# The last layer's two attentions as one stream of 32 tiles, with its norms and MLP weights made inside the stream

## What is computed

```python
def _L3_xattn_ref(hidden_states, encoder_states, ltor_mask, cross_mask, ln1_s, ...):
    ln_out = layernorm(hidden_states, ln1_s, ln1_b)
    qkv = ln_out @ w_qkv + b_qkv
    q, k, v = jnp.split(qkv, 3, axis=-1)
    ctx = merge_heads(attention(split_heads(q), split_heads(k), split_heads(v), ltor_mask))
    x = hidden_states + ctx @ w_ao + b_ao
    ln_out = layernorm(x, ln2_s, ln2_b)
    q = ln_out @ w_q + b_q
    kv = encoder_states @ w_kv + b_kv
    k, v = jnp.split(kv, 2, axis=-1)
    ctx = merge_heads(attention(split_heads(q), split_heads(k), split_heads(v), cross_mask))
    x = x + ctx @ w_co + b_co
    ln_out = layernorm(x, ln3_s, ln3_b)
    return x + gelu(ln_out @ w1 + b1) @ w2 + b2
```

## Time and profile before

| | |
|---|---|
| median of three runs | 1942.26 us (1941.73 to 1946.75) |
| the profiled execution | 1941.19 us, span from first to last instruction 1939.5 us |
| mean granted clock of PE | 0.942 of full |
| busy: PE, PEld, DVE, ACT, POOL | 89%, 76%, 52%, 51%, 22% |
| layer 3 begins, its MLP begins, the span ends | 1510.1, 1824.2, 1939.5 us |

### The profile page before, as it was taken

One profiled execution on the slowest core, in us unless ns is written; L12 is line 12 of the kernel. 1 busy time (PEld: TensorE's weight loads), 2 busy tenths in 40 slices (PEclk: granted clock), 3 DMA queues, 4 the chain that ended last, 5 costly groups with the idle time before them and its releaser, 6 DMA issues. The chain is left out here.

```text
span 1939.5 us, 36373 instructions
## 1 busy us (share of the span) xinstructions
PE 1731.0 (89%) x14350; PEld 1470.4 (76%) x14350; DVE 1002.6 (52%) x2150; ACT 998.8 (51%) x1890; POOL 431.9 (22%) x399
## 2 busy tenths in 40 slices
PE   5999999999979999999998598899489689699597
PEld 4888889888858888898887488577366467567486
DVE  6444444444364444444443733677678566667633
ACT  4545555455435555555554344566457476476443
POOL 5000000000020000000000300345510377377400
PEclk7999999999979999999999799899789799799799
DMA  4000000000020000000000100000100000100101
GB/s 153 23 22 22 0 22 22 22 22 0 1 67 23 22 22 0 22 22 22 22 0 1 47 0 8 21 2 2 52 1 0 26 2 2 36 2 2 47 0 44
DMA packets 55049, 39.77 MB, mean 21 GB/s; under 512 B 11891, under 2 KB 54451, under 8 KB 54963
## 3 DMA queue, kind: packets, MB, share of 16 engines
q1 hardware_dynamic: 54962, 38.57, 6.7%
HBM read 36.46 MB, written 2.10 MB: 20 GB/s over the span
## 5 line engine op out<-in xcount | busy, mean ns | idle before, releaser
L689 DVE TENSOR_TENSOR l0a_c_lo<-l0a_c_ps,l0a_c_hi 128x512 fp32r<-128x512 f32 x128 | 88.6, 692 | 267.2 <-ACT l0a_c_hi L643 267.2
L631 ACT ACTIVATE l0a_weight_t<-l0a_t_ps 64x256 f32<-64x256 f32 x256 | 96.8, 378 | 230.7 <-PE l0a_t_ps L532 229.2
L728 DVE TENSOR_TENSOR x<-l0a_o_ps,x 128x1024 f32<-128x1024 f32 x64 | 78.4, 1225 | 202.9 <-PE l0a_o_ps L102 202.9
L552 PEld LDWEIGHTS l0a_c_ps<-l0a_weight_t,l0a_v 128*128 128x128 f32 x1024 | 135.3, 193 | 14.4 <-ACT l0a_weight_t L631 3.0
L100 PE MATMUL l0a_o_ps<-l0a_wo_hi,l0a_c_hi 128*128 128x256 f32 x512 | 144.2, 282 | 0.0
L101 PE MATMUL l0a_o_ps<-l0a_wo_lo,l0a_c_hi 128*128 128x256 f32 x512 | 143.8, 281 | 0.0
L102 PE MATMUL l0a_o_ps<-l0a_wo_hi,l0a_c_lo 128*128 128x256 f32 x512 | 143.7, 281 | 0.0
L102 PE MATMUL l0a_v_ps<-l0a_wv_hi,ctx_lo 128*128 128x256 f32 x512 | 143.6, 280 | 0.0
L100 PE MATMUL l0a_v_ps<-l0a_wv_hi,ctx_hi 128*128 128x256 f32 x512 | 143.6, 280 | 0.0
L101 PE MATMUL l0a_v_ps<-l0a_wv_lo,ctx_hi 128*128 128x256 f32 x512 | 143.0, 279 | 0.0
L552 PE MATMUL l0a_c_ps<-l0a_weight_t,l0a_v 128*128 128x128 f32 x1024 | 136.9, 277 | 1.7 <-ACT l0a_weight_t L631 1.7
(11 more groups left out here) (426 smaller groups left out, 4877.5 us busy)
## 6 DMA issues: line engine op xcount, KB each, us to landing
l0a_raw<-in_L_xattn_wq_dram SPq DMA_DIRECT2D x32, 128.0 KB, 2.3
l0a_raw<-in_L_xattn_wk_dram SPq DMA_DIRECT2D x32, 128.0 KB, 2.3
l0a_raw_v<-in_L_xattn_wv_dram SPq DMA_DIRECT2D x16, 256.0 KB, 3.3
l0a_raw_o<-in_L_xattn_wo_dram SPq DMA_DIRECT2D x32, 128.0 KB, 2.8
l0a_wo_all<-in_L_xattn_wo_dram SPq DMA_DIRECT2D x2, 2048.0 KB, 8.3
ctx_rows<-in_ctx_dram SPq DMA_DIRECT2D x4, 512.0 KB, 5.7
x<-in_x_dram SPq DMA_DIRECT2D x4, 512.0 KB, 8.9
l0m_raw<-in_L_xattn_w_fc_dram SPq DMA_DIRECT2D x2, 1024.0 KB, 5.5
```

Source lines behind the costliest of these rows:

```text
L552: last = pe.matmul(by_tile[:, m, b, :, :], v[(j - HP) // HP % 2][:, m * HB + b, p * K:(p + 1) * K], weight_t[:, m, b, :, :].rearrange("p a ...
L631: last = act.activation(weight_t[half, :, :, a, :], t_ps[half, 0:GT // 2 * P] .rearrange("p (m b q) -> p m b q", b=HB, q=SEQ), ACT.Copy)
L689: dve.tensor_tensor(c[p][1][:], c_ps[:], c[p][0][:].bitcast(F32), ALU.subtract).then_inc(c_lo, 1)
L728: dve.tensor_tensor(chip.x[:, rows, :], o_ps[:], chip.x[:, rows, :], ALU.add).then_inc(added, 1)
```

## The change

`narrow_attention` takes a list of phases. Layer 3 calls it once with both attentions, 32 tiles T (tile T % 16 of phase T // 16); the slots run over 32 tiles and the tail has one slot more. Layer 1 calls it with one phase, and its instructions stay as they were.

- One `turn_input` with `bare=True`: the rows are normalised and transposed without scale and offset, `whole` falls away, `h_lo` is subtracted from PSUM. `phase_weights` (the old hooks moved out, called for each phase) puts the scale into the weights' rows (ACT and DVE in two halves) and the offset into the bias columns, with two more matmuls for each column; POOL's hook runs once.
- The norms before the second attention and before the MLP are made in the stream, for two tiles at a time (`normed_pair`, slots 7, 9, ..., 37): `gather` on DVE and `spread_of_pair` on POOL in the slot before, `norm` on DVE between `find_top` and `mask_scores`, `turn_normed` on PE between `turn_rows`/`values` and `project`, `take_normed` on ACT, `rest_of_normed` on DVE. They go through bank a, whose next `turn` now waits for `h_lo_done`.
- The MLP's weights are loaded and split in the stream's last slots (`mlp_weights`; its `k` is s - 32): w1_hi on ACT in slot 32, w2_hi on ACT in 33, w2_lo on POOL in 34, b1 columns on PE and w1_lo on DVE in 35. `dense_mlp` gets them and has no preparation.

```diff
-def turn_input(chip, tag, scale=None, offset=None, beside=None):
+def turn_input(chip, tag, scale=None, offset=None, beside=None, bare=False):
...
-                            pe.wait_ge(whole_done if norm else lo_done, (g - TB) * CH + c + 1)
+                            pe.wait_ge(whole_done if scaled_norm else lo_done, (g - TB) * CH + c + 1)
...
-                pool.wait_ge(b2_in, 16)
+                if not prepared:
+                    pool.wait_ge(b2_in, 16)
...
+def mlp_weights(chip, tag, w1, b1, w2, b2, norm, keep, LAST):
...
+            for free, count in found["free"]:
+                sp.wait_ge(free, count)
+            sp.dma_start(raw1, w1.rearrange("(c p) n -> p c n", p=P)).then_inc(w1_in, 16)
+            sp.dma_start(raw2, w2.rearrange("(f p) n -> p f n", p=P)).then_inc(w2_in, 16)
...
+        def scalar(act, k):
+            if k == 0:
+                act.wait_ge(w1_in, 16)
+                act.wait_ge(small_in, 64)
+                for c in range(CH):
+                    last = act.activation(w1_hi[:, c, :], raw1[:, c, :], ACT.Copy, scale=gain[:, 0, c:c + 1])
+                last.then_inc(w1_hi_done, 1)
+            if k == 1:
+                act.wait_ge(w2_in, 16)
+                act.activation(w2_hi, raw2, ACT.Copy).then_inc(w2_hi_done, 1)
+
+        def gpsimd(pool, k):
+            if k == 2:
+                pool.wait_ge(w2_hi_done, 1)
+                pool.tensor_tensor(w2_lo, raw2, w2_hi.bitcast(F32), ALU.subtract).then_inc(w2_lo_done, 1)
+
+        def tensor(pe, k):
+            if k == LAST:
+                pe.wait_ge(*found["bank_free"])
+                pe.wait_ge(w1_in, 16)
+                pe.wait_ge(small_in, 64)
+                for f in range(FC):
+                    own = slice(f * P, (f + 1) * P)
+                    pe.matmul(bank[:, f:f + 1], b1_row[0:1, own], chip.one[0:1, 0:1], start=True, stop=False)
+                    for c in range(CH):
+                        last = pe.matmul(bank[:, f:f + 1], raw1[:, c, own], gain[:, 1, c:c + 1], start=False, stop=c == CH - 1)
+                last.then_inc(b1_made, 1)
+
+        def vector(dve, k):
+            if k == LAST:
+                dve.wait_ge(b1_made, 1)
+                dve.tensor_copy(b1_cols[:], bank[:, 0:FC]).then_inc(b1_ready, 1)
+                dve.wait_ge(w1_hi_done, 1)
+                for c in range(CH):
+                    dve.scalar_tensor_tensor(w1_lo[:, c, :], raw1[:, c, :], gain[:, 0, c:c + 1], w1_hi[:, c, :].bitcast(F32),
+                                             ALU.mult, ALU.subtract)
...
+    def normed_pair(s):
+
+        t = added_tile(s - 1) if s > 0 else None
+        return t // 2 if t is not None and t % 2 == 1 and (t < TILES - NT or following) else None
...
+                    if T >= NT:
+
+                        pool.wait_ge(normed_done, (T - NT) // 2 + 1)
...
+                def spread_of_pair(m):
+
+                    two = slice(m % (NT // 2) * 2, m % (NT // 2) * 2 + 2)
+                    pool.wait_ge(ln_gathered, m + 1)
+                    pool.tensor_scalar(ln_spread[:, two], chip.x_moments[:, two, 1], 1e-5, None, ALU.add).then_inc(ln_spread_done, 1)
+                    pool.wait_ge(ln_spread_done, m + 1)
+                    pool.tensor_tensor(ln_inverse[:, two], ln_spread[:, two], chip.minus_half[:].to_broadcast([P, 2]),
+                                       ALU.pow).then_inc(ln_inverse_done, 1)
...
+                            if turned_before(s):
+                                pe.wait_ge(h_lo_done, turned_before(s))
...
+                def turn_normed(m, c):
+
+                    pe.wait_ge(turned_taken[0], min(c + 1, CHUNKS))
+                    pe.wait_ge(normed_done, m + 1)
+                    if m > 0:
+                        pe.wait_ge(h_lo_done, m)
+                    for x in range(CH):
+                        for a in range(2):
+                            last = pe.transpose(bank_a[:, (x * 2 + a) * P:(x * 2 + a + 1) * P], normed[:, a, x * P:(x + 1) * P], chip.ident[:])
+                    last.then_inc(normed_turned, 1)
...
+                def norm(m):
+                    dve.wait_ge(ln_inverse_done, m + 1)
+                    if m > 0:
+                        dve.wait_ge(normed_turned, m)
+                    for a in range(2):
+                        t = (2 * m + a) % NT
+                        last = dve.tensor_scalar(normed[:, a, :], chip.x[:, t, :], chip.x_moments[:, t, 0:1], ln_inverse[:, t:t + 1],
+                                                 ALU.subtract, ALU.mult)
+                    last.then_inc(normed_done, 1)
...
                     if multiply and 0 <= s - 1 < CHUNKS:
                         find_top(s - 1)
+                    if normed_pair(s) is not None:
+                        norm(normed_pair(s))
                     if s < CHUNKS:
                         mask_scores(s)
                     if done is not None:
                         rest_of_rows(done)
                     if not multiply and s < CHUNKS:
                         find_top(s)
+                    if normed_pair(s + 1) is not None:
+                        gather(normed_pair(s + 1))
+                    if normed_pair(s) is not None:
+                        rest_of_normed(normed_pair(s))
                     if job is not None and job[0] == "q":
                         take_queries(bank_b, job[1], job[2])
+                    if "vector" in extra:
+                        extra["vector"](dve, s - CHUNKS)
...
+            if k in normed:
+                for c in range(CH):
+                    last = pe.matmul(cols_ps[:, i:i + 1], src[:, c, x * P:(x + 1) * P], gain[:, 1, c:c + 1], start=False, stop=c == CH - 1)
```

More of the change, by code:

```diff
@@ L244, in _ @@
             def _(act):
-                if norm:
+                if scaled_norm:
                     act.wait_ge(gain_in, 32)
@@ L785, in dense_mlp @@
             turn_input(chip, f"{tag}h", scale, offset, dict(sync=sync, gpsimd=gpsimd, tensor=tensor, vector=vector))
+        if not prepared:
+            with ExitStack() as before:
+                prepare(before)
         hidden = [sb(f"hidden{b}", [P, GN]) for b in range(2)]
@@ L852, in _ @@
                     chunk(0, f)
-                    if f == 0:
+                    if f == 0 and not prepared:
                         act.wait_ge(w2_in, 16)
@@ L910, in narrow_attention @@
+def narrow_attention(chip, tag, heads, kv_heads, phases, score_scale, multiply, before, beside=None, following=False):
     nc = chip.nc
@@ L926, in narrow_attention @@
     NV = BV + CH
-    mask_tiles = 1 if multiply and mask.shape[0] == 1 else NT
     chip_h = (chip.h_hi, chip.h_lo)
-    crossed = CROSSED_CONTEXT and source[0] is chip.ctx_hi
     PARTS = KB * PER
+    NGS = PH * NG
     GS = GT * CT
@@ L1061, in tensor @@
             def tensor(pe):
-                pe.wait_ge(bias_spread, 1)
-                for i in range(NV):
-                    last = pe.matmul(cols_ps[:, i:i + 1], bias_rows[0:1, i, :], chip.one[0:1, 0:1], start=True, stop=True)
-                last.then_inc(bias_turned, 1)
-                pe.wait_ge(bv_spread, 1)
-                for c in range(CH):
-                    last = pe.matmul(cols_ps[:, D:2 * D], bv_wide[:, c, :], raw_o[:, c, :], start=c == 0, stop=c == CH - 1)
-                last.then_inc(bv_used, 1)
@@ L1117, in narrow_attention @@
-            turn_input(chip, f"{tag}h", *norm, beside=dict(sync=sync, gpsimd=gpsimd, tensor=tensor, scalar=scalar, vector=vector))
+                for p in prepared:
+                    p["tensor"](pe)
+            def scalar(act):
+                for p in prepared:
+                    p["scalar"](act)
+            def vector(dve):
+                for p in prepared:
+                    p["vector"](dve)
+            before(dict(sync=sync, gpsimd=gpsimd, tensor=tensor, scalar=scalar, vector=vector))
@@ L1155, in made_before, with turned_before @@
             return (QB if what == "q" else KB) + sum(1 for i in range(s) if (j := job_of(i)) and j[0] == what)
+        def turned_before(s):
+            return sum(1 for i in range(s) if normed_pair(i) is not None)
         def part(m, g, engine_in):
@@ L1431, in _ @@
                 for s in range(SLOTS):
-                    done, job = ended_tile(s), job_of(s)
+                    done, job, added = ended_tile(s), job_of(s), added_tile(s)
                     if done is not None:
                         normalise(done)
-                    if s > 0 and ended_tile(s - 1) is not None:
-                        add_output(ended_tile(s - 1))
+                    if added is not None:
+                        add_output(added)
                     if multiply and 0 <= s - 1 < CHUNKS:
                         find_top(s - 1)
+                    if normed_pair(s) is not None:
+                        norm(normed_pair(s))
                     if s < CHUNKS:
```

448 lines of the change are left out of this document (295 added, 153 removed).

## The result

The changed kernel takes **1969.14 us** (median of 4, 1967.73 to 1971.02) against 1941.99 before (4 runs, 1937.96 to 1946.75): ratio **1.0142**, 95% interval 1.0125 to 1.0159. It is 27 us slower; the forecast was 1941, no change, with a range from 1923 to 1951.

The account below looks back on a forecast made before the run. PE was taken as the bound by a hair in slots with projections, POOL's 6.25 us loop in light ones. Terms -54.3 + 40.8 + 13 + 1.5 - 2.2 = -1.2 us gave 1941.1 from 1942.3; range 1923 to 1951.

Parts of the forecast that it names:

- PE then waits 2.27 + 2.15 - 2.19 = 2.23, plus 0.44: 2.67 per pair: Normed slots: PE's wait for norm plus four transposes cost 2.67 us, so a pair of slots takes 15.38.
- whole stream is the forecast's: Layer 3's merged stream, first mask to mask of tile 31: 226.7 us against 185.95 before, +40.8.
- the profile shows 0.5 after each pause of PE: Argument against the rival of PE at the high clock in preparation and b1 matmuls (1934 us, chance 0.1).
- the b1 columns: Tail: 48 PE records take 5.4 us at the high level, 10.7 at the low; 7.5 taken.
- The tail's term: From the mask of tile 31 to the MLP: 40.3 us against 38.84 before, so +1.5 and nothing won.
- Output of tile 31: Tail: the output of the last tile ends at +24.2 us after its mask.
- The preparation: Before the stream, both attentions' weights made together: +13 us, with DVE last and columns at clock 0.5.
- The lock: Normed slots: POOL's shift shuts out norm's second half on DVE, so norm ends 2.1 us after the maximum, not 0.7.
- That shift isn't lengthened: Normed slots: POOL slips between norm's two operations and its 1.90 us shift isn't lengthened; by the skill page, 0.25 us wait.
- The rival, norm not shut out: Normed slots: norm's two operations hold together, PE waits 0.83 us; 18 us faster, about 1924; chance 0.2.
- POOL would set slots 28 to 31: Stream's end without projections: POOL's loop of 6.25 us sets the pace, 21.4 us in all.
- its slower rival: POOL's bo_row (0.69 us) also goes ahead of norm's second half in thirteen slots: +8, about 1949.5; chance 0.15.

Follow-up runs that it names:

- The first experiment: Changed kernel with PE's wait at turn_normed filled with 20 transposes of the identity (slots up to 30): 1953.12 us, 1.0057 of the kernel before.
- experiment 7: Changed kernel with PE's waits ahead of turn_normed in slots 33, 35 and 37 filled with 28, 38 and 50 transposes: 1964.93 us, ratio 1.0115 to the kernel before.
- experiment 6: Changed kernel with only the MLP weights' loads, splits and b1 columns moved to other places in the last slots: 1955.70 us, ratio 1.0075 to the kernel before.
- experiment 9: Changed kernel with norm on ACT, the MLP weights' work moved and the attentions' preparation reordered: 1917.01 us, ratio 0.9867 to the kernel before.
- experiment 3: Changed kernel with norm's two DVE operations taking the inverse as a second tensor instead of a scalar: 1969.05 us, ratio 1.0145 to the kernel before.
- experiment 5: Changed kernel with norm made by ACT (two activations with scale and bias columns) instead of DVE: 1926.82 us, ratio 0.9925 to the kernel before.
- experiment 10: As experiment 9, but b1's columns at the ends of slots 31 to 35, w2_hi on ACT and w2_lo on POOL in slot 33: 1922.29 us, ratio 0.9894.

## Why the prediction was wrong

**What failed** is one step: "PE then waits 2.27 + 2.15 - 2.19 = 2.23, plus 0.44: 2.67 per pair". The wait was right (2.23 forecast, 2.16 in the bracket). From the slot's start to the first transpose of norm PE took 4.61 us (1685.98 to 1690.59), 2.42 more than the 2.19 at which it used to be there. But I priced everything behind the wait at the high level. From the first of these transposes to the next slot took 5.35 us; at the high level it is 0.44 + 3.42 (1747.63 to 1751.05 in the earlier trace rows), 3.86. So the pair pays 2.42 + 0.44 + 1.49 = 4.35, measured 17.01 - 12.71 = 4.30. Eleven pairs from mask 6 to mask 28 came to 186.52 us, forecast 169.2. The first experiment leaves the wait and takes the low level away: its eleven pairs take 169.3 us, its whole stream is the forecast's to 0.6 us.

The row was there: the earlier trace rows has clock 0.5 behind a wait of 3.47 us, and I wrote that the profile shows 0.5 after each pause of PE. I used it for the preparation and the b1 columns and not for the slot in which the change itself made a pause. As a reading it also went too far: the other row stands behind a wait of 2.68 us and ran at 1.00.

**The tail's term** (40.3, measured 49.2) has the same cause in part. Filling its waits won 4.7 of the 8.9 us, and by the estimate above the last fill itself cost some 2.5. I took 7.5 us for the b1 columns, in the middle of two bounds; they took 11.7, all at the low level and above my upper bound (10.7, from the 0.222 a record of the earlier trace rows; 0.243 here). Started at the high level, in experiment 7, they took 8.7. Output of tile 31 ended at +28 instead of +24. The order of the rest was as forecast: norm of pair 14 took 4.27 us beside w2_lo, and w1_lo stood ahead of add_output. Experiment 6 shows what these places cost: without them the stretch is 16.5 us shorter, and 3.4 of these were spent again between masks 28 and 31 (26.2 us instead of 22.7).

**The preparation** (+13, measured +15.4): mechanism right. DVE stood 8.55 us until PE had made the first columns, at the low level. Experiment 9 shows that 6 of these 15 us were order, not work.

**The lock** was right for the second half of norm: 1.96 us (2.31 less one of 0.35). That shift isn't lengthened was wrong by a little: shift took 2.00 us in every slot with a norm behind the maximum and 1.90 or 1.91 in the others. By the Trainium skill, "SBUF — State Buffer", section "SBUF: two separate sides", shift also has to wait for the rest of norm's first half. The traces are nearer to that than to my reading: the second half began 0.16 us after shift (1688.50 against 1688.34) and shift was 0.09 longer; in experiment 3 it began 0.22 after it and shift took 2.07. The copy of the earlier trace rows, at 1442.18, had nothing to wait for: the second half there began at 1442.17. The rival, norm not shut out, fell in both forms tried on DVE (one tensor, and two in experiment 3). bo_row did not slip ahead of it. That POOL would set slots 28 to 31 was right only in part: with the slow stretch behind the wait of slot 29 they took 22.7, forecast 21.4; experiment 1, without it, has 21.9.

**The range** stopped at 1951 because its slower rival was bo_row's 0.69 us a slot. "It waits and then it is slow" would have been the rival: 12 x 1.5 = 18 us in the stream alone (slots 7 to 29), and 245.4 against 227.3 us is what experiment 1 found.

## What to carry to other kernels

A wait put into a matmul stream can cost twice: its length, here 2.4 us, and the low level behind it, here 1.5; price what stands behind it at both levels, with the spacings of rows at either. Before a small norm is put between a maximum and the next mask on DVE, look at what POOL is released to do by the same event; ACT was the free place here (1926.8 against 1969.1 us). Keep runs of one-column matmuls out of a stretch whose level matters: 1.9 and 2.6 us of them had the low level behind them. What was hidden in a wait has to be paid when the wait is removed.

## What was not expected of the hardware

- 2.16 us without work, once in two slots, had the granted clock at 0.5 for some 3.5 us behind it, though it was 1.00 in the wait itself; 0.36 and 0.86 us did not. In between the length alone does not tell: in slot 29, a wait of 1.67 us had 0.62 over the 4 us behind it in experiment 5, and in experiment 10 one of 1.69 us had an attention product of 1.13 us behind it, as at the high level.
- Transposes of 128 columns in the wait kept it (1.00), and 50 in a row brought it back from 0.50; matmuls of one column, busy for 1.87 of 1.90 us, did not keep it, and 11.7 us of them in a row stayed at 0.50. So did 15 us of matmuls with 128 repeated columns.
- Which property of the work counts was not settled. The matmuls that failed to keep or raise the level load weights for each short record, most of them 128 x 128, but so do the transposes.
